# Turning q and k by transposing transfers, and a new order of the weighted sum, the output projection and the sampling

## The chip, the cores and the metric

One core of one Trainium2 chip runs the whole program. The metric is the device time of one execution in microseconds (us). The kernel before took 1519.93 us, the median of 3 runs (1518.76 to 1524.53).

## What is computed

64 sequences of 64 steps and 512 features go through four stages in a row, each added to the running x:

```python
# 1, attention over each sequence, 16 heads of 32
xn = rms_norm(x, g_norm) * (1 + scale) + shift       # scale, shift = cond @ W_emb + b_emb
q, k, v = split_heads(xn @ W_qkv)
q = rms_norm(q, g_q); k = rms_norm(k, g_k)
o = softmax(q k^T * 32**-0.5) v                      # the weighted sum
x = x + o + o @ W_out                                # the output projection
# 2, sampling: between neighbouring features, at positions made from cond,
#    one row of 512 for each of the 64 sequences
i0 = floor(ix); w1 = ix - i0
x = x + (1 - w1) * x[..., i0] + w1 * x[..., i0 + 1]
# 3, a GRU over the steps, and 4, an oscillator (Runge-Kutta, 4 evaluations with a
#    512 x 512 coupling a step) driven by x: 64 steps, one after another
```

## The kernel before, in words

**Stages.** Attention and sampling come first, in `attention_and_sampling`; the two recurrences follow in `recurrences` and are not touched. The 64 sequences are taken in 32 pairs of 128 tokens. Every matrix product is made of float16 pairs (a high and a low part), in three terms, high by high, high by low, low by high; the sampling, whose matrix holds only zeros and ones, has two.

**Slots.** Work is pipelined by hand. Slot i has a fixed list on each engine, in which `pair(d)` is pair i + d: the projections are those of pair i (q, k and v in three banks of psQ), the scores and the softmax those of pair i - 1, the weighted sum and the output projection those of i - 2, and the sampling that of i - 3 (called tap). Slots 0 to 30 are of this kind; the last pair, N0, and what is left of N1 to N3 come after, in lists of their own. Engines meet only at semaphores.

**TensorE (PE)** in a slot (line 1284): `turn_qk` of pair i - 1, eight transposes of 128 x 128 float32 from qn into psA (line 1119); `project` q; `scores`; `project` k; `mix` of the first element (the weighted sum, line 1208); one chunk in four of `project` v; `mix` of the second element; three chunks of `project` v; `proj`, the output projection (line 1228), which writes the bank psO that `mix` wrote; `sample` twice, once for each element of the pair (line 1176); and `turn_rs`, which lays the norms of x along the columns for `scale_x`. `sample` writes psQ's bank 0 or 1, waits for the one-hot matrix (`e_built`), for q's or k's bank to be read out (`qn_done`), and for the copies of x1 (`x1_moved`).

**x1** (one buffer, but for the last three pairs) holds a pair's x after attention, as float16 high and low part, and a second time moved by one row, since sampling takes two neighbouring rows. ACT writes the high part (`high_x1`, line 617), POOL the low part (`low_x1`, line 442), once both samplings of the pair before are through. SP then makes the copy that is moved by one row with three transfers: 112 rows, 15 rows, and the last row from the next chunk (`move_x1`, line 290).

**DVE** (`slot`, line 970) is the busiest of the others: it scales x (`scale_x`, line 756), takes the low part of q and k out of psA (`low_qk`, line 746), builds the one-hot matrices by comparing the positions, broadcast to all partitions, with each partition's index (`build`, line 763, eight instructions of 512 columns a slot), sums squares, takes the least score (`least`), makes the norm exact by one step of Newton's method (`newton`), scales q and k into qn (`scale_qk`, line 801), takes low parts, and weighs the sampled taps (`weigh_taps`, line 858).

**ACT** casts and squares, takes logarithm and exponential for norms and softmax, and writes the high parts (`high_qk`, line 530, with the gain as its scale).

**POOL** (line 463) in a slot: `modulate` of pair i + 1 behind DVE's `scale_x`; `add_taps` of pair i - 4, twice two additions; `low_x1`; `low_x`; then, behind DVE's reciprocals, `norm_p` and `low_halves` of pair i - 1.

**SP** issues the transfers in this order (line 333): `turn_p` twice, transposing transfers that turn the softmax weights of pair i - 2, 128 x 1024 float16 each, in place of work on PE; x of pair i + 3 in two layouts; the first row of positions; `move_x1`; a piece of W_hh or W_ih; the second row. A transfer that waits holds up all behind it.

**Start.** SP first loads cond turned, W_emb, x, cond as it is, then W_qkv. DVE's first work on cond as it is (`grid_front`, line 894, the sampling positions) stands in its list ahead of splitting W_emb into parts (`low_we`).

Of the kernel before, what the change touches and what calls it, by code (L numbers as in the profile page):

```python
# [16 lines left out]
PART = 128  # L17
# [45 lines left out]
def program(nc, x, x_turned, cond, cond_turned, vectors, W_emb, W_qkv, W_out, W_ih, W_hh, coupling_turned, out, rows_dram, wih_dram):  # L63
# [8 lines left out]
    with ExitStack() as ctx:  # L72
# [26 lines left out]
        with ExitStack() as s:  # L99
            attention_and_sampling(nc, ctx, s, block, banks, S, x2_done, x2_first, ts_, first4, XR, condT, ident, Wx, later, x, x_turned, cond, cond_turned,  # L100
                                   vectors, W_emb, W_qkv, W_out, W_ih, W_hh, coupling_turned, rows_dram, wih_dram)
# [4 lines left out]
def attention_and_sampling(nc, sems, ctx, block, banks, S_, x2_done, x2_first, ts_, first4, XR, condT, ident, Wx, later, x, x_turned, cond, cond_turned,  # L106
                           vectors, W_emb, W_qkv, W_out, W_ih, W_hh, coupling_turned, rows_dram, wih_dram):
# [29 lines left out]
    lidx, gqk = sb("lidx", [PART, KC]), sb("gqk", [PART, 1])  # L137
# [12 lines left out]
    qkT = first4[:, :, :, :].rearrange("p a c b -> p (a c b)").bitcast(F16).rearrange("p (i v c n) -> p i v c n", i=2, v=2, c=KC)  # L150
# [3 lines left out]
    S = sb("S", [PART, HEADS, T])  # L154
    mn = sb("mn", [PART, HEADS])
# [5 lines left out]
    rows = [sb(f"rows{u}", [PART, D], F16) for u in range(2)]  # L161
# [18 lines left out]
    i0h = rows[0][0:B, :]  # L180
# [14 lines left out]
    def last_use(eng, p):  # L195
        if p.n == N2.n:
            eng.wait_ge(rs_T, NP)
        elif p.n == N1.n:
            eng.wait_ge(qkv_done, NP * 3)
        else:  # L200
            eng.wait_ge(qk_T, NP)
# [13 lines left out]
    cond_in, condT_in, vectors_in = sem("cond_in"), sem("condT_in"), sem("vectors_in")  # L215
# [17 lines left out]
    qk_T, qk_hi, qk_ready = sem("qk_T"), sem("qk_hi"), sem("qk_ready")  # L233
    sc_done, mn_done, sub_done, exp_done, den_done, rden_done, p_done = (
# [44 lines left out]
    def _(sp):  # L279
# [37 lines left out]

        def store_wih(k):
# [14 lines left out]
        def slot(pair, i):  # L333
# [5 lines left out]
            if i == 2:  # L339
                sp.wait_ge(rows_ready, 1)  # L340
                sp.dma_start(rows_dram, i0h).then_inc(rows_out, 16)
# [14 lines left out]
            if p := pair(-2):  # L356
                load_rows(p, 1)

# [24 lines left out]
    def _(pool):  # L383
# [4 lines left out]
        nc.gpsimd.iota(lidx[:, :], pattern=[[PART, KC]], base=0, channel_multiplier=1,  # L388
# [127 lines left out]
    def _(act):  # L516
# [3 lines left out]
        act.dma_start(vT[:, :], vectors).then_inc(vectors_in, 16)  # L520
        nc.scalar.add_instruction(mybir.InstLoadActFuncSet(name=nc.get_next_instruction_name(), act_func_set_id=LN_EXP_SET))
# [111 lines left out]
        def slot(pair, i):  # L633
            if p := pair(-1):
                high_qk(p, 0)
                high_qk(p, 1)
# [14 lines left out]
            if p := pair(1):  # L651
                high_x(p)
            if i == 1:
                high_cp(1)
                high_wo(0)
                high_wo(1)
            if i > 0:
# [8 lines left out]
            if p := pair(-1):  # L666
                if p.n > 1:
                    exps(p, 2, HEADS)
                    high_halves(p, 0)
                else:  # L670
                    exps_at_once(p)
# [5 lines left out]
            if 0 <= i - WR_FROM < WR_PIECES:  # L677
                high_wr(i - WR_FROM)
            if p := pair(-1):
# [28 lines left out]
        high_qk(N1, 0)  # L708
        high_qk(N1, 1)
# [5 lines left out]
        high_qk(N0, 0)  # L715
        high_qk(N0, 1)
# [24 lines left out]
    def _(dve):  # L741
# [4 lines left out]
        def low_qk(p, n):  # L746
            dve.wait_ge(qk_hi, p.n * 2 + n + 1)
            need(dve, sc_done, p.n)
            t = psA[:, n, :].rearrange("p (c n) -> p c n", c=KC)
            if n == 0:  # L750
                v.scalar_tensor_tensor(out=qkT[:, 1, 0, :, :], in0=t, scalar=gqk[:, 0:1],
                                       in1=qkT[:, 0, 0, :, :], op0=ALU.mult, op1=ALU.subtract)
            else:
                v.tensor_tensor(qkT[:, 1, 1, :, :], t, qkT[:, 0, 1, :, :], ALU.subtract).then_inc(qk_ready, 1)
# [8 lines left out]
        def build(p, b, chunks):  # L763
            if chunks[0] == 0:
                dve.wait_ge(rows_in[b], p.n * 16 + 16)
                if p.n < NP - 1:
                    need(dve, samp_done, p.n * 2 + b - 1)
                elif b == 1:
                    for u in range(2):
                        dve.wait_ge(wih_out[u], 3 * KC // 2 * 16)  # L770
                if p.n == 0:
                    dve.wait_ge(consts, 3)
                    dve.wait_ge(cp_lo, KC)
                    dve.wait_ge(wo_lo, KC)
            for k in chunks:
                e = v.tensor_scalar(E_of(p, b)[:, k, :], rows[b][:, :], lidx[:, k:k + 1], None, ALU.is_equal)  # L776
            if chunks[-1] == KC - 1:
                e.then_inc(e_built, 1)
# [22 lines left out]
        def scale_qk(p):  # L801
            dve.wait_ge(rs_step, (p.n + 3) * STEPS)
            need(dve, qk_T, p.n)
            for n in range(2):
# [1211 lines left out]
```

## Time and profile before

| | |
|---|---|
| median of 3 runs | 1519.93 us |
| the profiled execution | 1523.93 us, span 1522.1 us, TensorE clock 0.994 of full |
| PE matmul busy | 1474.8 us (97%) |
| DVE | 1309.1 us (86%) |
| ACT | 900.4 us (59%) |
| POOL | 762.2 us (50%) |
| POOL's normalisation of the softmax (line 434), mean of 64 | 1.049 us |
| DMA, mean | 55 GB/s, busy in the first 16 of 40 slices |

The span is the time from the first to the last instruction of the profiled execution. An engine's busy time is a share of all stages together; attention and sampling end at about 600 us. Line 518 is ACT's helper for every activation, so that its groups are told apart by tiles. "first" is the tile first4, in which qkT lies; "front" holds x, the squares, the halves and xn; "room" holds the one-hot matrices; "um" the weighed taps.

### The profile page before, as it was taken

The numbers are of one execution on the slowest core, as the hardware profiler recorded it, in microseconds if no ns is written. First come the engines' busy times: TensorE is split into PE (matmuls) and PEld (weight loads), VectorE is DVE, ScalarE is ACT, GpSimd is POOL, SyncE is SP. The second block draws the span as 40 slices with busy tenths as digits, with TensorE's granted clock in tenths as the row PEclk, the third lists the DMA queues.
The fourth block names the chain that finished last, engine by engine and source line by source line (L and its number), as shares of the span: only waits on it lengthen the run. The fifth ranks groups of instructions, "written<-read, shape, count | busy, mean of one in ns | idle before, by whom it ended". The sixth has DMA issues, their size and how long they took to land.

```text
span 1522.1 us, 95000 instructions
## 1 busy us (share of the span) xinstructions
PE 1474.8 (97%) x42214; PEld 1306.2 (86%) x42214; DVE 1309.1 (86%) x3190; ACT 900.4 (59%) x2753; POOL 762.2 (50%) x916
## 2 busy tenths in 40 slices
PE   4899999999999999999999999999999999999997
PEld 2466776667766678999999999999999999999996
DVE  6898888888888887698888888888889888988887
ACT  5566766667666653555555555555555555555553
POOL 2567676776777655443443444344444444434432
PEclk9999999999999999999999999999999999999999
DMA  7255444545455441000000000000000000000000
GB/s 256 55 124 108 108 103 108 118 116 125 120 128 129 93 128 54 8 16 15 12 15 15 15 12 15 15 12 15 15 12 16 15 15 12 15 15 12 15 15 14
DMA packets 122602, 84.03 MB, mean 55 GB/s; under 512 B 68656, under 2 KB 107824, under 8 KB 122192
## 3 DMA queue, kind: packets, MB, share of 16 engines
q1 hardware_dynamic: 121968, 77.87, 20.4%
q8 instruction: 331, 5.42, 1.5%
q14 instruction: 79, 0.65, 0.2%
q10 hardware_dynamic: 224, 0.09, 0.0%
HBM read 42.23 MB, written 11.60 MB: 35 GB/s over the span
## 4 chain that ended last, share of the span: by engine, by line
PE 90%; DVE 4%; issue 2%; POOL 1%; ACT 1%; DMA 0%; SPq 0%; DVEq 0%; ACTq 0%; POOLq 0%
PE psB L1435 34%; PE psA L1464 15%; PE psQ L1146 15%; PE psA L1469 8%; PE psQ L1189 7%; PE psO L1235 5%; PE psO L1223 2%; PE psA L1124 2%; PE psB L1171 2%; POOL S L434 1%; DMA front<-in_cond 0%; DVE psO L1648 0%; DVE den L835 0%; POOL front L453 0%; DVE room L880 0%
## 5 line engine op out<-in xcount | busy, mean ns | idle before, releaser
L1435 PE MATMUL psB<-first,Wx 128*128 128x64 f16 x9216 | 291.3, 193 | 1.7 <-issue 1.1
L1464 PE MATMUL psA<-ts,Cp 128*128 128x64 f16 x8160 | 280.9, 193 | 6.9 <-ACT ts L1535 6.2
L1435 PE MATMUL psB<-first,Whh 128*128 128x64 f16 x9072 | 286.4, 193 | 1.1 <-POOL first L1900 0.5
L1435 PEld LDWEIGHTS psB<-first,Wx 128*128 128x128 f16 x9216 | 278.5, 98 | 2.4 <-issue 1.9
L1146 PE MATMUL psQ<-Wx,front 128*128 128x512 f16 x1152 | 275.0, 385 | 4.3 <-DVE front L952 4.1
L1435 PEld LDWEIGHTS psB<-first,Whh 128*128 128x128 f16 x9072 | 273.9, 98 | 1.8 <-issue 1.1
L1464 PEld LDWEIGHTS psA<-ts,Cp 128*128 128x128 f16 x8160 | 256.3, 98 | 8.3 <-ACT ts L1535 7.0
L1535 ACT ACTIVATE ts<-qst 128x256 f16<-128x256 f32 x192 | 80.1, 417 | 297.1 <-DVE qst L1648 297.1
L1146 PEld LDWEIGHTS psQ<-Wx,front 128*128 128x128 f16 x1152 | 106.7, 99 | 120.6 <-issue 7.7
L1900 POOL TENSOR_TENSOR en<-rz,dn 128x256 f32<-128x256 f32 x64 | 46.7, 729 | 259.5 <-issue 256.7
L1469 PE MATMUL psA<-ts,Cp 128*128 128x64 f16 x4080 | 161.4, 193 | 0.3 <-issue 0.3
L1675 DVE TENSOR_TENSOR ts<-psA,ts 128x256 f16<-128x256 f32 x255 | 107.3, 421 | 47.0 <-ACT psA L1535 47.0
L776 DVE TENSOR_SCALAR room<-rows,lidx 128x512 f16<-128x512 f16 x256 | 144.8, 608 | 0.3
L434 POOL TENSOR_TENSOR S<-S,rden 128x512 f32<-128x512 f32 x64 | 67.0, 1049 | 151.2 <-DVE rden L844 151.2
L1469 PEld LDWEIGHTS psA<-ts,Cp 128*128 128x128 f16 x4080 | 137.0, 98 | 0.6 <-issue 0.4
L518 ACT ACTIVATE S<-psB,mn 128x64 f32<-128x64 f32 x448 | 133.2, 339 | 1.2 <-DVE mn L822 1.2
L1648 DVE SCALAR_TENSOR_TENSOR rest<-cub,psQ 128x256 f32<-128x256 f32 x256 | 106.6, 416 | 7.3
L1648 DVE SCALAR_TENSOR_TENSOR psO<-qst,psO 128x256 f32<-128x256 f32 x253 | 107.1, 423 | 2.1
L1189 PE MATMUL psQ<-x,room 128*128 128x128 f16 x1856 | 108.5, 219 | 0.0
L1189 PEld LDWEIGHTS psQ<-x,room 128*128 128x128 f16 x1856 | 104.9, 98 | 0.1
L518 ACT ACTIVATION_READ_ACCUMULATOR S<-psB,mn 128x1 f32 x448 | 104.4, 233 | 0.0
L1900 POOL TENSOR_TENSOR V<-X3b,first 128x256 f32<-128x256 f32 x64 | 46.9, 733 | 114.2 <-DVE first L1762 113.0
(194 smaller groups left out, 2879.0 us busy)
## 6 DMA issues: line engine op xcount, KB each, us to landing
front<-in_x SPq DMA_DIRECT2D x32, 256.0 KB, 3.1
XR<-in_x_turned SPq DMA_DIRECT2D x32, 256.0 KB, 3.4
rows<-rows_dram SPq DMA_DIRECT2D x64, 128.0 KB, 3.0
out<-ob SPq DMA_DIRECT2D x63, 128.0 KB, 1.7
x<-x SPq DMA_DIRECT2D x29, 224.0 KB
Whh<-in_W_qkv SPq DMA_DIRECT2D x12, 256.0 KB, 7.8
room<-in_W_hh SPq DMA_DIRECT2D x12, 256.0 KB, 2.9
room<-in_W_ih SPq DMA_DIRECT2D x12, 256.0 KB, 2.8
```

The lines of the kernel that those rows point to most:

```text
L434: nc.gpsimd.tensor_tensor(part, part, rden[:, 8 * h:8 * h + 8].unsqueeze(2).broadcast_to([PART, HEADS // 2, T]), ALU.mult)\
L518: return nc.scalar.activation(out, in_, f, **k)
L776: e = v.tensor_scalar(E_of(p, b)[:, k, :], rows[b][:, :], lidx[:, k:k + 1], None, ALU.is_equal)
L1146: last = mm(psQ[:, n, :], xn[p.u][:, i, c, :], Wqkv[:, j, c, n * D:(n + 1) * D], start=(c == 0 and t == 0), stop=(c == KC - 1 and t == 2))
L1189: last = mm(o[:, m, :, :], E_of(p, b)[:, c, m * PART:(m + 1) * PART], x1_of(p)[:, :, i, c, b, :], start=(c == 0 and i == 0), stop=(c == KC ...
L1435: last = mm(o, W_[:, i, c, g * PART:(g + 1) * PART], src[:, j, c, :], start=False, stop=False, skip_group_check=True)
L1464: mm(psF[:, s % 2, m, :], Cp[:, i, c, m * PART:(m + 1) * PART], ts_[:, 0, c, :], start=(c == 0 and m == 0 and i == 0), stop=False, skip_gr ...
L1469: last = mm(psF[:, s % 2, m, :], Cp[:, 0, c, m * PART:(m + 1) * PART], ts_[:, 1, c, :], start=False, stop=(c == KC - 1), skip_group_check= ...
L1535: return nc.scalar.activation(out, in_, f, **k)
L1648: return v.scalar_tensor_tensor(out=flat(out), in0=flat(in0), scalar=scalar, in1=flat(in1), op0=ALU.mult, op1=op1)
L1675: v.tensor_tensor(ts_[:, 1, :, :], th, ts_[:, 0, :, :], ALU.subtract).then_inc(S["ts_ready"], 1)
L1900: return nc.gpsimd.tensor_tensor(flat(out), flat(in0), flat(in1), op)
```

## The change

- **q and k.** DVE now scales q and k into psA rather than qn and multiplies q by a row of gains (new tile `gain_row`); ACT and DVE take high and low part from there into qkh (the room of qn), still in the order of tokens; and SP turns each half with a transposing transfer at the end of its list. PE's `turn_qk` is left for the last pair alone, with `high_qk_turned` and `low_qk_turned`, the old forms.
- **PE's order.** Both `mix` move behind three chunks of v's projection (the second with the fourth chunk ahead of it), and `sample` of the first element comes ahead of `proj`.
- **DVE's and ACT's order.** `low_qk` moves from the next slot to the end of its own; `weigh_taps` of the first element goes ahead of it; `low_wr` and `high_wr` move to the middle of the slot, builds and exponentials are regrouped.
- **One-hot matrices.** The row of positions is kept twice, the second less 128, so that one instruction of 1024 columns builds what two did: four a slot. The row's transfer grows from 128 to 256 KB.
- **Start.** cond as it is comes by ACT's queue, with the gains broadcast to all partitions (128 x 4 KB) ahead of it; DVE's `grid_front` and `gains` wait for all three transfers of that queue.

```diff
@@ SP
         def load_rows(p, b):
             need(sp, e_built, p.n * 2 + b - 1)
-            sp.dma_start(rows[b][:, :], rows_dram[bass.ds(p.n * 2 + b, 1), :].rearrange("a n -> (a n)")
-                         .partition_broadcast(PART)).then_inc(rows_in[b], 16)
+            sp.dma_start(rows[b][:, :, :].rearrange("p c n -> p (c n)"), rows_dram[bass.ds(p.n * 2 + b, 1), :, :]
+                         .rearrange("a c n -> (a c n)").partition_broadcast(PART)).then_inc(rows_in[b], 16)
...
+        def turn_qk(p, n):
+            sp.wait_ge(qk_low, p.n * 2 + n + 1)
+            need(sp, sc_done, p.n)
+            sp.dma_start_transpose(qkT[:, n, :, :, :].rearrange("p i c n -> p (i c) n"), qkh[:, n, :, :].rearrange("p i n -> p (i n)"))\
+                .then_inc(qk_in, 16)
...
             if p := pair(-2):
                 load_rows(p, 1)
+            if i < NP - 1:
+                turn_qk(pair(0), 0)
+                turn_qk(pair(0), 1)
...
-                sp.dma_start(condtok, cond).then_inc(cond_in, 16)
@@ ACT
+        act.dma_start(gains2.rearrange("p v n -> p (v n)"), gains.rearrange("v n -> (v n)").partition_broadcast(PART)).then_inc(vectors_in, 16)
+        act.dma_start(condtok, cond).then_inc(vectors_in, 16)
...
         def high_qk(p, n):
-            act.wait_ge(qk_T, p.n + 1)
-            need(act, sc_done, p.n)
-            o, t = qkT[:, 0, n, :, :], psA[:, n, :].rearrange("p (c n) -> p c n", c=KC)
+            act.wait_ge(qn_done if n else q_gained, p.n * 2 + 2 if n else p.n + 1)
+            need(act, qk_in, p.n * 32)
+            a(qkh[:, n, 0, :], psA[:, n, :]).then_inc(qk_hi, 1)
...
-            if (p := pair(-1)) and p.n > 1:
-                exps(p, 0, 2)
-            if p := pair(-2):
-                high_o(p)
+            if p and p.n > 1:
+                exps(p, 4, 8)
             guess(i + 2, QK_X if pair(2) else QK)
...
+            if p and p.n > 1:
+                exps(p, 8, 13)
+            if p2 := pair(-2):
+                high_o(p2)
+            if p and p.n > 1:
+                exps(p, 13, HEADS)
+            high_qk(pair(0), 0)
+            if p and p.n > 1:
+                high_halves(p, 0)
...
+            high_qk(pair(0), 1)
@@ DVE
         def low_qk(p, n):
             dve.wait_ge(qk_hi, p.n * 2 + n + 1)
+            v.tensor_tensor(qkh[:, n, 1, :], psA[:, n, :], qkh[:, n, 0, :], ALU.subtract).then_inc(qk_low, 1)
...
+            for k in range(2):
+                e = v.tensor_scalar(E_of(p, b)[:, 2 * k:2 * k + 2, :].rearrange("p c n -> p (c n)"), rows[b][:, :, :].rearrange("p c n -> p (c n)"),
+                                    lidx[:, k:k + 1], None, ALU.is_equal)
+            e.then_inc(e_built, 1)
...
+        def scale_qk(p, ns=range(2)):
             dve.wait_ge(rs_step, (p.n + 3) * STEPS)
-            need(dve, qk_T, p.n)
-            for n in range(2):
-                v.tensor_tensor(qn[:, n, :].rearrange("p (h d) -> p h d", d=DH), psQ[:, n, :].rearrange("p (h d) -> p h d", d=DH),
+            to = sq if p.n == NP - 1 else psA
+            for n in ns:
+                v.tensor_tensor(to[:, n, :].rearrange("p (h d) -> p h d", d=DH), psQ[:, n, :].rearrange("p (h d) -> p h d", d=DH),
                                 rs[:, n * HEADS:(n + 1) * HEADS].unsqueeze(2).broadcast_to([PART, HEADS, DH]), ALU.mult)\
                     .then_inc(qn_done, 1)
+                if n == 0 and p.n < NP - 1:
+                    dve.wait_ge(qn_done, p.n * 2 + 1)
+                    v.tensor_tensor(psA[:, 0, :], psA[:, 0, :], gain_row[:, :], ALU.mult).then_inc(q_gained, 1)
...
         def grid_front():
-            dve.wait_ge(cond_in, 16)
+            dve.wait_ge(vectors_in, 48)
...
             if tap:
-                build(tap, 0, (1, 2, 3) if tap.n > 0 else range(KC))
+                build(tap, 0)
...
+            if 0 <= i - WR_FROM < WR_PIECES:
+                low_wr(i - WR_FROM)
+            if tap:
+                build(tap, 1)
             sums_qk(qk, 1)
             means(cols, qk, x)
...
+            newton(i + 2, cols)
+            scale_qk(qk, range(1))
+            if (p := pair(-1)) and p.n > 1:
+                invert_sum(p, 0)
             if p := pair(-2):
                 low_o(p)
-            newton(i + 2, cols)
-            scale_qk(qk)
+            scale_qk(qk, range(1, 2))
...
             if tap:
-                build(tap, 1, (2, 3))
+                weigh_taps(tap, 0)
+            low_qk(qk, 0)
+            low_qk(qk, 1)
@@ PE
         def slot(pair, i):
-            if p := pair(-1):
-                turn_qk(p)
             project(pair(0), 0)
...
             if p := pair(-2):
+                project(pair(0), 2, range(KC - 1))
                 mix(p, 0)
-                project(pair(0), 2, range(1))
+                project(pair(0), 2, range(KC - 1, KC))
                 mix(p, 1)
-                project(pair(0), 2, range(1, KC))
-                proj(p)
             else:
                 project(pair(0), 2)
             if p := pair(-3):
                 sample(p, 0)
+            if p := pair(-2):
+                proj(p)
+            if p := pair(-3):
                 sample(p, 1)
             if p := pair(2):
                 turn_rs(p)
```

In the changed kernel each engine's list still ends with what belongs to the second sampling: DVE's slot ends with `low_v` and `weigh_taps` of the second element, and the next one begins with `scale_x`. POOL's list and the place of `move_x1` in SP's are as before.

## Rows read from the trace of the kernel before

**Rows 1.** Busy time by stretch: from:to, length, each engine's busy time (count), clock, DMA share, GB/s.

```profile
315.28:332.46 17.18, 17.18 (x352) 12.24 (x350) 14.96 (x29) 11.75 (x47) 12.04 (x13) 1.00 0.50 125
...
0.00:38.20 38.20, 16.21 (x136) 9.43 (x136) 23.30 (x45) 19.87 (x38) 8.49 (x18) 0.91 0.75 255
```

**Rows 2.** PE in order of time, slot at 315 us: start, length, instructions, idle before.

```profile
311.70 3.74 PE L1189 MATMUL psQ<-x,room 128*128 128x128 f16 x64
...
315.39 1.04 PE L1124 MATMUL psA<-ident,qn 128*128 128x128 f32 x8
...
316.26 2.75 PE L1146 MATMUL psQ<-Wx,front 128*128 128x512 f16 x12
...
326.21 2.84 PE L1235 MATMUL psO<-oT,Wo 128*128 128x128 f16 x48
...
328.89 3.74 PE L1189 MATMUL psQ<-x,room 128*128 128x128 f16 x64
```

**Rows 3.** DVE in order of time, the same slot.

```profile
315.48 0.69 DVE L847 TENSOR_TENSOR um<-psQ,WT 128x512 f32<-128x512 f32 x1
...
316.09 0.68 DVE L760 TENSOR_TENSOR front<-XR,psB 128x512 f32<-128x512 f32 x1
...
318.45 2.30 DVE L776 TENSOR_SCALAR room<-rows,lidx 128x512 f16<-128x512 f16 x3
```

**Rows 4.** POOL in order of time, the same slot.

```profile
316.84 1.09 POOL L453 TENSOR_TENSOR front<-front,modA 128x512 f32<-128x512 f32 x1 [0.45 <-DVE front L760]
...
322.09 1.15 POOL L447 TENSOR_TENSOR x<-XR,x 128x512 f16<-128x512 f32 x1
...
330.85 2.73 POOL L440 TENSOR_TENSOR front<-S,front 128x512 f16<-128x512 f32 x2
```

**Rows 5.** SP's issues in order of time, that slot and the one at 538 us.

```profile
323.27 1.51 SPq L300 DMA_DIRECT2D x<-x  x2
...
538.35 2.66 SPq L315 DMA_TRANSPOSE PT<-front  x2
...
546.75 1.51 SPq L300 DMA_DIRECT2D x<-x  x2
...
548.30 0.64 SPq L302 DMA_DIRECT2D x<-x  x1
```

**Rows 6.** Busy time by stretch, behind the issues at 538.35 and 546.75.

```profile
542.50:543.00 0.50, 0.50 (x71) 0.50 (x73) 0.50 (x2) 0.47 (x1) 0.50 (x2) 1.00 0.00 0
...
549.80:550.00 0.20, 0.20 (x7) 0.20 (x5) 0.18 (x1) 0.20 (x3) 0.00 (x0) 1.00 0.07 10
...
550.20:550.40 0.20, 0.20 (x7) 0.20 (x5) 0.20 (x1) 0.20 (x3) 0.00 (x0) 1.00 0.00 0
```

**Rows 7.** DMA issues of the whole run: count, KB, us to landing.

```profile
rows<-rows_dram SPq DMA_DIRECT2D x64, 128.0 KB, 3.0
...
out<-ob SPq DMA_DIRECT2D x63, 128.0 KB, 1.7
```

**Rows 8.** Line 776 (build), slots from 60 to 560 us: shortest, median, longest in ns.

```profile
L776 DVE TENSOR_SCALAR room<-rows,lidx x228: 300/533/1449, 75.7 to 559.9; 128x512 f16<-128x512 f16 x114
```

**Rows 9.** DVE and ACT in order of time, the start.

```profile
12.14 0.42 DVE L896 TENSOR_SCALAR um<-front 64x512 f32<-64x512 f32 x1 [7.86 <-DMA front<-in_cond]
...
15.86 2.34 DVE L880 SCALAR_TENSOR_TENSOR room<-Wo,room 128x1024 f16<-128x1024 f32 x2
...
9.57 1.06 ACT L518 ACTIVATE room<-Wo 128x1024 f16<-128x1024 f32 x1 [0.27 <-DMA Wo<-in_W_emb]
```

**Rows 10.** PE in order of time, slots 2 and 3.

```profile
58.22 1.10 PE L1171 MATMUL psB<-first 32*64 32x64 f16 x96 [2.87 <-DVE first L754]
...
59.25 4.45 PE L1146 MATMUL psQ<-Wx,front 128*128 128x512 f16 x12
...
75.83 1.09 PE L1171 MATMUL psB<-first 32*64 32x64 f16 x96 [1.56 <-DVE first L754]
```

**Rows 11.** Busy time by stretch, slot 2.

```profile
59.80:63.80 4.00, 4.00 (x35) 1.43 (x36) 3.96 (x5) 0.27 (x1) 3.92 (x4) 0.63 1.27 158
```

More of the change, by code:

```diff
@@ L60, in need, with program @@
     eng.wait_ge(sem, value)
-def program(nc, x, x_turned, cond, cond_turned, vectors, W_emb, W_qkv, W_out, W_ih, W_hh, coupling_turned, out, rows_dram, wih_dram):
+def program(nc, x, x_turned, cond, cond_turned, vectors, gains, W_emb, W_qkv, W_out, W_ih, W_hh, coupling_turned, out, rows_dram, wih_dram):
     B, T, D = x.shape
@@ L100, in program @@
             attention_and_sampling(nc, ctx, s, block, banks, S, x2_done, x2_first, ts_, first4, XR, condT, ident, Wx, later, x, x_turned, cond, cond_turned,
[L101 removed]
+                                   vectors, gains, W_emb, W_qkv, W_out, W_ih, W_hh, coupling_turned, rows_dram, wih_dram)
         with ExitStack() as s:
@@ L106, in attention_and_sampling @@
 def attention_and_sampling(nc, sems, ctx, block, banks, S_, x2_done, x2_first, ts_, first4, XR, condT, ident, Wx, later, x, x_turned, cond, cond_turned,
-                           vectors, W_emb, W_qkv, W_out, W_ih, W_hh, coupling_turned, rows_dram, wih_dram):
+                           vectors, gains, W_emb, W_qkv, W_out, W_ih, W_hh, coupling_turned, rows_dram, wih_dram):
     B, T, D = x.shape
@@ L160, in attention_and_sampling @@
     x1 = sb("x1", [PART, 2, 2, KC, 2, T], F16)
-    rows = [sb(f"rows{u}", [PART, D], F16) for u in range(2)]
+    rows = [sb(f"rows{u}", [PART, 2, D], F16) for u in range(2)]
     um = [sb(f"um{u}", [PART, KC, 2, T]) for u in range(2)]
@@ L656, in slot @@
                 high_wo(1)
+            p = pair(-1)
+            if p and p.n > 1:
+                exps(p, 0, 4)
             if i > 0:
@@ L761, in scale_x, with build @@
                             rsT.unsqueeze(1).broadcast_to([PART, KC, PART]), ALU.mult).then_inc(xr_done, 1)
[L763 to L778, printed above, removed]
+        def build(p, b):
+            dve.wait_ge(rows_in[b], p.n * 16 + 16)
+            if p.n < NP - 1:
+                need(dve, samp_done, p.n * 2 + b - 1)
+            elif b == 1:
+                for u in range(2):
+                    dve.wait_ge(wih_out[u], 3 * KC // 2 * 16)
+            if p.n == 0:
+                dve.wait_ge(consts, 3)
+                dve.wait_ge(cp_lo, KC)
+                dve.wait_ge(wo_lo, KC)
+            for k in range(2):
+                e = v.tensor_scalar(E_of(p, b)[:, 2 * k:2 * k + 2, :].rearrange("p c n -> p (c n)"), rows[b][:, :, :].rearrange("p c n -> p (c n)"),
+                                    lidx[:, k:k + 1], None, ALU.is_equal)
+            e.then_inc(e_built, 1)
         def means(cols, qk, x):
@@ L917, in grid_rows @@
             dve.wait_ge(grid_step, 8)
-            v.tensor_copy(i0h, i0).then_inc(rows_ready, 1)
+            for c in range(2):
+                last = v.tensor_scalar(i0h[:, c, :], i0, 1.0, float(-c * PART), ALU.mult, ALU.add)
+            last.then_inc(rows_ready, 1)
         def grid_weight():
@@ L2002 @@
         vectors=np.concatenate(vectors, axis=0).T,
+        gains=np.stack([np.tile(inputs[n], D // inputs[n].shape[0]) for n in ("L0_cond_g_q", "L0_cond_g_k")]),
         W_emb=inputs["L0_cond_W_emb"], W_qkv=inputs["L0_cond_W_qkv"], W_out=inputs["L0_cond_W_out"],
```

112 lines of the change are left out of this document (49 added, 63 removed).

## The prediction

> **What bounds the kernel now.** I read the page first: its slices show TensorE (PE) in the nineties almost throughout, and the DMA engines busy only in the first 16 slices of 38 us, where attention and sampling run; the recurrences behind are not touched. Then the busy time by stretch: in one steady slot of the attention stage (one pair of batch elements, 17.18 us) PE is busy for all 17.18 us, DVE for 14.96, ACT for 11.75 and POOL for 12.04, at the full clock [rows 1]. So the slot is PE's, and what PE sheds counts only as long as nothing else then takes longer. For that I followed one slot on each queue [rows 2 to 5]. S marks the end of a slot's second sampling, 315.44 us (311.70 plus 3.74 in [rows 2]).
>
> **The loop to watch** is that of x1, which has one buffer. From S: DVE weighs the last taps (315.48) and scales x (316.09) [rows 3]; POOL starts to modulate at 316.84, adds four taps, and subtracts for x1 from 322.09 to 323.24 [rows 4]; SP issues three copies of x1 one row down, the first at 323.27 [rows 5]; when all have landed PE may sample, which frees the buffer for the next pair. In the kernel before, PE samples at 328.89, 13.45 us behind S, and never waits.
>
> **The change part by part.**
>
> **PE loses the turning of q and k.** From 315.39 to 316.26 it costs 0.87 us a slot [rows 2]. The rest of the slot keeps its matmuls: 17.18 - 0.87 = 16.31 us.
>
> **The copies of x1 now gate PE.** Ahead of the first sampling stood projections, scores, weighted sum and output projection; the output projection (326.21 to 328.89, 2.68 us) now comes behind it. Everything else that stood ahead took 316.26 to 326.21, 9.95 us, and the next slot's project now begins 0.05 us ahead of S (316.26 less 0.87, against 315.44). So PE reaches the sampling 9.9 us behind S. The copies: SP issues the first 323.27 - 315.44 = 7.83 us behind S, as POOL's list is not changed. How long they take no view lists, so I bound it. In a quiet slot the first is issued at 546.75 and the third at 548.30 [rows 5]; the last packets of the three pass in 549.8 to 550.2 [rows 6], 3.05 to 3.45 us behind the first issue. From an issue to landing the quickest transfer of the kernel, the output's, takes 1.7 us and the positions' 3.0 [rows 7]; behind the third issue (1.55) that makes 3.25 to 4.55. I take 4.05, towards the upper end, since in most slots weight loads stand in the same queue. Copies landed: S + 7.83 + 4.05 = S + 11.9, and 0.1 for PE to start. Then both samplings, 3.74 with the tail of the last matmul, with the output projection's 2.68 between them: 6.42 us. The loop is 7.83 + 4.05 + 0.10 + 6.42 = **18.40 us** a slot, against 17.18: +1.22. With the bounds 3.25 and 4.55 it is 17.60 to 18.90. PE has some 2.1 us idle in each slot, and the 0.87 us are worth nothing. The loop closes from slot 3 to slot 30, 27 times: 27 x 1.22 = **+32.9 us** (+11 to +46).
>
> **A second loop of the same length** has POOL in it: DVE now waits for the first sampling (weighing its taps) ahead of the low parts of q and k and the second reciprocal, and behind that reciprocal POOL has a normalisation, 1.05 by the table above, and two subtractions, 2.73 us [rows 4]. From the start of the first sampling: 1.95 for it, 0.6 x 3 on DVE, 0.3 for reciprocal and start, 3.8 on POOL, 7.85 in all; modulation comes at 6.42 + 1.40 = 7.82. It adds nothing, but a faster copy alone would not undo the loss.
>
> **Two transposing transfers a slot on SP,** at the end of its list. A pair of the same size (the weights of attention) is issued from 538.35 for 2.66 us and the data is through by 542.5 [rows 5, 6], 4.2 us on; added SP time 2.7 us a slot, on a queue with 8 us of issues in 17. Queued behind are the next slot's transfers: the pair for the weighted sum (due 8 us into the slot) and loads that are due a slot later. From the start of the first sampling: 1.95 for it, 0.6 for its taps and 0.6 for the low part of q, then the first issue at 3.2 and both halves there at 3.2 + 4.2, some 7.5 us behind the start; scores need them 6.4 + 2.7 = 9.1 behind. Cover 1.6 us, and 2.1 more of PE's idle time. Cost 0. If the cover went, each us late would be a us a slot. Against this stands a rule: by the Trainium skill (VectorE: DVE Perf Modes, The three transpose paths) a transfer takes 1309 ns to turn a 128 x 128 block of 2 bytes and TensorE 390, and TensorE is to be preferred where PSUM will do; with 8 blocks a half, one after another, the slot would be set by turning. This trace disagrees: 16 blocks pass in about 3 us beside others.
>
> **DVE.** One multiplication more (the gain, 128x512 out of PSUM, as the 0.68 of L760 [rows 3]); one of the low parts a little shorter (-0.07); it has 2.2 us idle a slot before and more after. Building the one-hot matrices: 8 instructions of 512 columns become 4 of 1024. Three of them now take 2.30 us beside POOL [rows 3], though one takes 0.30 at its best and 1.45 at its worst [rows 8]: each seems to wait for POOL's current instruction. The Trainium skill (SBUF — State Buffer, SBUF: two separate sides) says that the two engines hold a shared pair of ports for a whole instruction: then half as many would wait half as often, and the first one, longer, could hold back POOL's modulation by 0.15 us, 4 us in all. Without it I put 0; the DVE way from S to the scaled q, with two builds more in it, sums to some 10.5 us behind S and so stays behind the copies' 11.9.
>
> **ACT** turns two reads of PSUM into two of the same kind: 0, under its 5.4 us of idle. Weights' casts moved earlier: 0, same reason. Rows' transfers double to 256 KB, still 3 us, needed 5 us later: 0.
>
> **The start.** DVE stands still until 12.14 us for cond's 128 KB, queued on SP behind the weights, and only then splits W_emb, done at 15.86 + 2.34 = 18.2 us; ACT had its last high part started at 9.57 [rows 9]. On ACT's queue cond lands early, but 512 KB of gains come along, 2 us at the 255 GB/s of this stretch [rows 1]. The split could end at 9.6 + 1.1 + 2 + 1.2 = 13.9: -4.3. W_qkv's pieces land for long after, so I take **-3** (-4.3 to +2).
>
> **Slots 1 and 2, and the end.** They are bound by chains of waits; transfers in place of 0.87 us of turning cost some 3 us more latency, DVE's order gives some back: 0 (-3 to +3). One turning goes from the last slots: **-0.9**.
>
> **Sum** against the profiled execution, 1523.9 us: +32.9 - 3 - 0.9 = +29 us, 1553. The median of the runs shown is 4 us lower, so **1549 us**, +1.9%; by the bounds of the terms 1524 to 1566.
>
> **The rivals.**
> **The kernel gets the PE time back.** If the copies land in 2.1 us rather than 4.05, PE is gapless at 16.31: 27 x -0.87 = -23.5, with start and end -27.4: **1492**. For it: the kernel before never waits for them. Against: the packets last 3 us at least, and the second loop. 0.18, with all mixtures.
> **It evens out.** The loop is at 17.2 to 17.35: copies at about 3 us, in the lower bound of the rows, with the start's gain against the rest: **1516 to 1525**. 0.14.
> **The clock falls in PE's pause.** The granted clock was 0.63 of the 2.4 GHz level in 59.8 to 63.8, so partly the 1.2 GHz one [rows 11], behind 2.87 us of waiting at 58.22; 75.83 came behind only 1.56 us [rows 10]. The 2.1 us lie between. A fall as long as that one would add about 1.7 us to each slot (project took 4.45 at 59.25 [rows 10] in place of 2.75 [rows 2]): 27 x 1.7 = 46, **1595**. 0.06.
> **The transfers that turn are slow.** Where a pair takes up to 3.7 us longer, the pause absorbs it. Three times the 4.2 us, 12.6, puts the halves at 15.8 behind the start of the sampling, 6.7 late, 2.1 of it covered: 27 x 4.6 = 124, **1673**. Against: the pair's 4.2 us held in a stretch with other transfers before and behind it [rows 6]. 0.02. The Trainium skill's figure above would make it 21 us a pair, further out still; this trace has no such row.
> **Forecast** 0.60: 18.40 us a slot, between 1526 and 1572.
>
> **How the numbers follow.** What measurement can tell from no change is about 0.5%, 7.6 us. Faster 0.18; same 0.14; slower 0.60 + 0.06 + 0.02 = 0.68. The range leaves out the lowest part of the faster case (0.13) and the two slow ones at the top (0.07): 1506 to 1574. Its own range of the likeliest case is 1526 to 1572.
>
> **What would show it.** Right: slots of about 18.4 us; in the list of waits PE's weight load for sampling (L1189's successor) idle some 2 us a slot for the transfer of x1, no wait of scores for q and k; DVE's work in the start done 3 us earlier. Wrong: PE at 99% in the steady slots with a period of 16.3 to 16.5, or PE's pause ahead of scores, or ahead of the output projection, or a granted clock under 1 in the steady stage.

## The result, and the profile after

| | before | after |
|---|---|---|
| median | 1520.68 us (4 runs, 1518.76 to 1524.53) | 1614.9 us (4 runs, 1613.15 to 1619.59) |
| ratio, with its 95% interval | | 1.0618 [1.0601, 1.0635] |
| the profiled execution: time, span | 1523.93, 1522.1 us | 1615.49, 1613.7 us |
| TensorE clock, share of full | 0.994 | 0.961 |
| PE, DVE, POOL busy | 1474.8, 1309.1, 762.2 us | 1493.5, 1307.2, 773.2 us |

The change costs 6.2%. The prediction said 1549 us (1506 to 1574): slower, as it was, but by 29 us where it was 94, and the range doesn't hold the result.

One steady slot, from S (the end of the second sampling) to the next S. Busy time by stretch, in the columns of [rows 1]:

```profile
302.87:323.79 20.92, 18.04 (x343) 13.05 (x342) 14.95 (x25) 11.88 (x47) 12.04 (x13) 0.92 0.55 136
```

It is 3.74 us longer than the slot of [rows 1]. PE stands idle for 2.88 us of it, and although it lost the turning it is busy longer, 18.04 us for 17.18, because the clock is at 0.92. DVE, ACT and POOL do as much as before. PE in order of time shows both:

```profile
311.59 0.82 PE L1168 MATMUL psQ<-Wx,front 128*128 128x512 f16 x3
312.35 0.55 PE L1248 MATMUL psO<-PT,Vt 64*32 64x64 f16 x48
315.77 3.55 PE L1214 MATMUL psQ<-x,room 128*128 128x128 f16 x32 [2.88 <-DMA x<-x]
319.14 2.86 PE L1260 MATMUL psO<-oT,Wo 128*128 128x128 f16 x48
321.84 1.95 PE L1214 MATMUL psQ<-x,room 128*128 128x128 f16 x32
```

There is one pause, ahead of the first sampling, and it ends with the transfer of x1. The two samplings are the same 32 matmuls; the first took 3.37 us until the next group began, the second, undisturbed, 1.78. So matmuls run at half pace behind the pause. In [rows 2] both samplings together took 3.74. PE's list of waits over 90 to 640 us (waited for: us in total, times, longest) names this pause and almost nothing else:

```profile
PE psQ L1214 <- DMA x<-x: 67.2, 27, 3.9
PE psB L1196 <- DMA first<-qn: 0.7, 1, 0.7
```

What stands ahead of the transfer, POOL in order of time:

```profile
304.27 1.22 POOL L465 TENSOR_TENSOR front<-front,modA 128x512 f32<-128x512 f32 x1 [0.85 <-DVE front L785]
...
308.13 1.18 POOL L437 TENSOR_TENSOR um<-um 128x256 f32<-128x256 f32 x1
...
310.14 1.33 POOL L459 TENSOR_TENSOR x<-XR,x 128x512 f16<-128x512 f32 x1
```

POOL starts 1.40 us behind S, as before, but takes 7.20 us to the end of `low_x1` (311.47), where it took 6.40 in [rows 4]. SP follows at once, and turns q and k later in the slot:

```profile
311.51 1.50 SPq L304 DMA_DIRECT2D x<-x  x2
313.05 0.64 SPq L306 DMA_DIRECT2D x<-x  x1
...
320.67 2.63 SPq L325 DMA_TRANSPOSE first<-qn  x2
```

From the first issue of the copies (311.51) to PE's start (315.77) it is 4.26 us in this slot; from slot to slot it lies between 3.3 and 4.9.

DVE in order of time, its four wide builds and the scaling of q, which is read out of psQ by 313.84, 10.97 us behind S:

```profile
304.11 1.67 DVE L800 TENSOR_SCALAR room<-rows,lidx 128x1024 f16<-128x1024 f16 x2
...
308.64 1.82 DVE L800 TENSOR_SCALAR room<-rows,lidx 128x1024 f16<-128x1024 f16 x2
...
313.14 0.70 DVE L829 TENSOR_TENSOR psA<-psQ,rs 128x512 f32<-128x512 f32 x1
```

**The account.** S of slot 3 is at 98.42 us (before: 90.41), that of slot 30 at 650.79 (before: 556.11). The early slots cost 8.0 us, the 27 loops (650.79 - 98.42) / 27 = 20.46 us each in place of 17.25, together 86.7 us, and what follows is 3.1 us shorter. 8.0 + 86.7 - 3.1 = 91.6, the difference of the spans. On average over the 27 loops SP issues the first copy 8.62 us behind S, PE begins to sample 3.90 us later, and from there to the next S it takes 7.94 us: 20.46 in all.

The early part in order of time, the first rows DVE and ACT, the others PE:

```profile
9.02 0.42 DVE L923 TENSOR_SCALAR um<-front 64x512 f32<-64x512 f32 x1 [4.62 <-DMA front<-in_cond]
...
11.73 1.06 ACT L530 ACTIVATE room<-Wo 128x1024 f16<-128x1024 f32 x1 [0.23 <-DMA Wo<-in_W_emb]
...
21.31 4.87 PE L1168 MATMUL psQ<-Wx,front 128*128 128x512 f16 x12 [4.07 <-DVE front L981]
...
42.90 1.49 PE L1196 MATMUL psB<-first 32*64 32x64 f16 x96 [3.29 <-DMA first<-qn]
...
73.54 4.40 PE L1260 MATMUL psO<-oT,Wo 128*128 128x128 f16 x48 [5.72 <-DVE oT L892]
...
90.38 3.52 PE L1214 MATMUL psQ<-x,room 128*128 128x128 f16 x32 [1.99 <-DMA x<-x]
```

DVE's work on cond comes at 9.02 rather than 12.14 [rows 9], while ACT's last part of W_emb starts at 11.73 rather than 9.57: the gains delay the weights. Then scores wait for turned q and k, and the output projection of slot 2 waits 5.72 us for DVE.

### The profile page after: what moved, and what is told of

It reads as the page before. It is cut to its first block, busy times and chain, and to the rows that moved or that the text cites. A ratio compares the mean times of both kernels' runs of the same rounds, so it can differ in the third digit from the quotient of the medians.

```text
span 1613.7 us, 94467 instructions
## 1 busy us (share of the span) xinstructions
PE 1493.5 (93%) x41966; PEld 1323.7 (82%) x41966; DVE 1307.2 (81%) x3095; ACT 904.3 (56%) x2753; POOL 773.2 (48%) x916
## 4 chain that ended last, share of the span: by engine, by line
PE 70%; POOL 13%; DVE 5%; DMA 4%; issue 3%; SPq 3%; ACT 1%; ACTq 0%; DVEq 0%; POOLq 0%
PE psB L1459 32%; PE psA L1488 14%; PE psQ L1214 9%; PE psA L1493 7%; PE psO L1260 6%; POOL front L465 4%; DMA x<-x 4%; POOL um L437 3%; SPq L304 3%; POOL XR L440 3%; POOL x L459 2%; DVE front L785 1%; PE psQ L1168 1%; DMA front<-in_cond 0%; POOL S L446 0%
## 5 line engine op out<-in xcount | busy, mean ns | idle before, releaser
L1214 PE MATMUL psQ<-x,room 128*128 128x128 f16 x1856 | 146.3, 252 | 70.0 <-DMA x<-x 70.0
L1214 PEld LDWEIGHTS psQ<-x,room 128*128 128x128 f16 x1856 | 136.8, 115 | 72.4 <-issue 72.3
L874 DVE TENSOR_TENSOR um<-psQ,WT 128x512 f32<-128x512 f32 (+1 forms) x66 | 44.4, 675 | 95.4 <-PE psQ L1214 92.0
L530 ACT ACTIVATE front<-S 128x512 f16<-128x512 f32 x60 | 37.8, 630 | 135.0 <-POOL S L446 134.8
L1260 PE MATMUL psO<-oT,Wo 128*128 128x128 f16 x1536 | 102.9, 233 | 6.0 <-DVE oT L892 6.0
```

Of the source, the lines that this page charges most:

```text
L530: return nc.scalar.activation(out, in_, f, **k)
L1214: last = mm(o[:, m, :, :], E_of(p, b)[:, c, m * PART:(m + 1) * PART], x1_of(p)[:, :, i, c, b, :], start=(c == 0 and i == 0), stop=(c == KC ...
L1260: last = mm(psO[:, m, :], Wo[:, i, c, m * PART:(m + 1) * PART], oT[:, j, c, :], start=(c == 0 and t == 0), stop=(c == KC - 1 and t == 2))
```

## The experiments

Each ratio below is to the kernel before, run beside it on the same chip. "A slot" is the mean of the 27 loops, from S of slot 3 to S of slot 30.

**1. The gate moved nearer: POOL's `low_x1` ahead of `add_taps`,** in the changed kernel.

```diff
@@ POOL
-            for b in range(2):
-                if p := pair(-4):
-                    add_taps(p, b)
...
                 low_x1(p)
+            for b in range(2):
+                if p := pair(-4):
+                    add_taps(p, b)
```

> The changed kernel, with POOL's low part of x1 ahead of the four additions of taps. Theory (the loop through x1, made longer by POOL's chain and by the clock): POOL's low part ends some 3.4 us earlier, at 5.2 behind the end of the second sampling, the copies have landed at 9.5, PE no longer waits for them. What then gates the first sampling is DVE's scaled q, at 11.0 behind: 11.1 + 6.42 = 17.5 us a slot in place of 20.5, a pause of 1.1 us, clock 1.00: 1614.9 - 27 x 3.0 = 1534 us. Rival (the transposing transfers slow the queue and PE waits for them one way or another): the pause moves ahead of the scores, slots of 19 us or more, 1575 us or more.

Measured 1591.01 us, ratio 1.0446 [1.0412, 1.0480], a slot 19.48 us. The gate did move: the copies no longer end the pause. But another wait stood right behind them, as PE's list of waits (90 to 640 us) shows ("psA L829" is DVE's scaled q):

```profile
PE psQ L1214 <- DVE psA L829: 50.0, 26, 3.0
PE psQ L1214 <- DMA x<-x: 4.7, 2, 2.5
```

DVE and PE in order of time, in a slot whose S is at 336.76:

```profile
341.86 1.22 DVE L918 SCALAR_TENSOR_TENSOR room<-room 128x512 f16<-128x512 f32 x1
...
348.77 2.36 PE L1214 MATMUL psQ<-x,room 128*128 128x128 f16 x32 [1.92 <-DVE psA L829]
```

The sampling writes the bank of psQ in which q was projected, and so waits for DVE to scale q out of it. This came 12.0 us behind S, hardly earlier than in the changed kernel (12.9 in the slot shown, 12.5 on average), and the clock still fell: in 200 to 500 us it was 0.93.

**2. The output projection back ahead of both samplings,** in the changed kernel.

```diff
@@ PE
-            if p := pair(-3):
-                sample(p, 0)
             if p := pair(-2):
                 proj(p)
             if p := pair(-3):
+                sample(p, 0)
                 sample(p, 1)
```

> The changed kernel, with the output projection ahead of both samplings again. Theory: the copies are hidden, but the output projection then waits for the low part of o, which DVE takes 12.3 us behind the end of the second sampling: 12.4 + 2.68 + 3.74 = 18.8 us a slot, 27 x 1.7 = 46 us less, 1569 us, with a pause of 2.3 us ahead of the output projection and a clock still under 1. Rival (the new order of PE alone is the fault): slots of 16.3 to 16.6 us, 1505 us or less.

Measured 1694.7 us, ratio 1.1107 [1.1085, 1.1129], a slot 23.13 us. It went far beyond what was expected. PE's waits (90 to 640 us):

```profile
PE psO L1260 <- DVE oT L892: 79.5, 24, 3.5
PE psB L1196 <- DMA first<-qn: 26.6, 23, 3.0
```

DVE in order of time:

```profile
331.26 0.69 DVE L874 TENSOR_TENSOR um<-psQ,WT 128x512 f32<-128x512 f32 x1 [6.95 <-PE psQ L1214]
```

DVE's list weighs the first sampling's taps ahead of the low parts of q and k and of all that follows. With the sampling late, DVE stands idle for 6.95 us, the halves are turned late, and scores wait. POOL's normalisation of the softmax comes late with it, and here it holds `modulate` back: that starts 3.6 us behind S, right behind POOL's two subtractions, in place of 1.4. And `low_o`, which makes the output projection's operand, stands so far down DVE's list that the projection waits up to 3.5 us for it in its earlier place. The orders of PE and of DVE belong together; one can't be judged with the other left as it is.

**3. The kernel before with nothing but the first sampling ahead of the output projection.**

```diff
@@ PE
                 project(pair(0), 2, range(1, KC))
-                proj(p)
...
                 sample(p, 0)
+            if p := pair(-2):
+                proj(p)
+            if p := pair(-3):
                 sample(p, 1)
```

> The kernel before, with the first sampling ahead of the output projection and nothing else. Theory: the loop through x1 is 7.83 + 4.25 + 6.42 = 18.5 us a slot, +1.3 x 27 = +35, 1556 us, with a pause of 1.3 us in which the clock stays at 1. Rival 1 (it takes the transposing transfers and the longer builds for the loop to bind): 1521 us as before. Rival 2 (the clock falls in a pause of any length): 20 us a slot, 1595 us.

Measured 1568.88 us, ratio 1.0282 [1.0256, 1.0308], a slot 18.84 us. So the loop binds without the transposing transfers and the longer builds, which rival 1 denied: this one change of PE's order makes a slot 1.59 us longer, where the whole change makes it 3.21 us longer. What ended PE's pause was the copies in 11 of the 27 slots and DVE's scaled q in 16: the two gates stand side by side here too. The run also shows both outcomes for the clock, in neighbouring slots:

```profile
331.67 3.37 PE L1189 MATMUL psQ<-x,room 128*128 128x128 f16 x32 [1.98 <-DMA x<-x]
334.83 3.09 PE L1235 MATMUL psO<-oT,Wo 128*128 128x128 f16 x48
...
351.93 1.95 PE L1189 MATMUL psQ<-x,room 128*128 128x128 f16 x32 [1.29 <-DVE qn L805]
```

Behind 1.98 us of waiting the sampling took 3.37 us, behind 1.29 us it took its usual 1.95.

**4. The pause filled:** eight matmuls of 512 columns ahead of PE's wait for x1, in the changed kernel. Their result is overwritten.

```diff
@@ PE, in sample
             pe.wait_ge(e_built, p.n * 2 + b + 1)
+            if b == 0 and p.n < N3.n:
+                pe.wait_ge(qn_done, (p.n + 3) * 2 + 1)
+                need(pe, um_done, p.n * 2 - 1)
+                for _ in range(8):
+                    mm(psQ[:, 0, :], Cp[:, 0, 0, 0:PART], Cp[:, 0, 0, :], start=True, stop=True)
```

> The changed kernel, with eight matmuls of 512 columns added ahead of the first sampling's wait for x1; their result is written over by the sampling. They fill some 1.8 us of PE's pause. Theory (the clock falls in the pause and makes the sampling and the output projection slower, inside the loop): clock back to 1.00, the first sampling 1.8 us again, slots of 8.64 + 4.26 + 6.42 = 19.3 us, 27 x 1.15 = 31 us less, 1584 us. Rival (the clock is not in the loop, the slots are long for another reason): 1615 us or more.

Measured 1588.35 us, ratio 1.0413 [1.0382, 1.0444], a slot 19.28 us. PE in order of time:

```profile
342.64 1.89 PE L1207 MATMUL psQ<-Cp 128*128 128x512 f16 x8 [1.11 <-issue]
344.58 1.96 PE L1219 MATMUL psQ<-x,room 128*128 128x128 f16 x32
```

Busy time over 200 to 500 us:

```profile
200.00:500.00 300.00, 282.74 (x5480) 188.15 (x5465) 232.88 (x390) 188.49 (x749) 193.45 (x188) 1.00 0.63 146
```

Useless work is added, and yet each slot is 1.18 us shorter, with the granted clock at 1.00 rather than 0.92. So the clock's fall is in the loop. But the added matmuls are a gate of their own. They may only start when q has been scaled out of its bank, 10.96 us behind S, and they take 1.8 us; in 21 of the 27 slots the sampling then starts with no wait for the copies at all, as in the slot whose S is at 235.34:

```profile
246.41 1.89 PE L1207 MATMUL psQ<-Cp 128*128 128x512 f16 x8 [1.11 <-issue]
248.13 1.95 PE L1219 MATMUL psQ<-x,room 128*128 128x128 f16 x32
```

On average PE begins to sample 12.86 us behind S, 0.34 later than in the changed kernel, and needs 6.42 us from there to the next S, where the changed kernel needs 7.94. The clock's fall is therefore 1.52 us a slot, 27 x 1.52 = 41 us of the loss, and this run gives back 1.52 - 0.34 = 1.18 of it. That the expected 19.3 us came out is in part luck: its 4.26 us for the copies came from one slot, the average is 3.90, and the added matmuls made up the difference.

**5. DVE's way to q shortened:** experiment 1, and `low_wr` moved from the middle of DVE's slot behind `low_v`.

```diff
@@ DVE
-            if 0 <= i - WR_FROM < WR_PIECES:
-                low_wr(i - WR_FROM)
             if tap:
                 build(tap, 1)
...
+            if 0 <= i - WR_FROM < WR_PIECES:
+                low_wr(i - WR_FROM)
```

> The kernel of e1_x1_low_first, with DVE's low part of the recurrent weights (line 918, 1.22 us between the least score and the builds) moved behind v's low part. In e1 the first sampling came 12.0 us behind the end of the second, at DVE's scaled q. Theory (what is left in the loop is DVE's chain to the scaled q, then the clock): the sums of squares of k start when ACT has them, at 7.1 in place of 8.0, so the scaled q is there at 10.6 to 11.0; the pause of PE falls from 2.5 to about 1.2 us, the clock stays at 1, slots of 10.9 + 6.4 = 17.3 us: 27 x 2.7 less than e1's 1591, 1518 us. Rival (the clock falls in shorter pauses too): 18.5 to 19 us a slot, 1550 to 1565 us.

Measured 1546.6 us, ratio 1.0145 [1.0119, 1.0171], a slot 17.68 us. PE's waits (90 to 640 us):

```profile
PE psQ L1214 <- DVE psA L829: 21.2, 20, 1.7
PE psQ L1214 <- DMA x<-x: 10.0, 8, 2.1
```

One of its pauses, in order of time:

```profile
337.82 1.95 PE L1214 MATMUL psQ<-x,room 128*128 128x128 f16 x32 [1.04 <-DVE psA L829]
```

Of experiment 1's 50 us behind DVE 21 are left, and behind 1.04 us of waiting the sampling takes its full-clock time, 1.95 us. One instruction of 0.75 to 1.22 us moved is worth 1.80 us a slot: the wait itself and the clock behind it. The kernel stays short of what was expected, since S of slot 3 is still at 97.3 us and some slots still wait longer (1.75 us at 109 us, with the clock down behind it).

**6. The turning kept, the order put back.** From experiment 5: transfers, wide builds, start and experiment 1's order of POOL stay; PE's order is that of the kernel before less the turning, and ACT's and DVE's follow it.

```diff
@@ PE
-                project(pair(0), 2, range(KC - 1))
                 mix(p, 0)
-                project(pair(0), 2, range(KC - 1, KC))
+                project(pair(0), 2, range(1))
                 mix(p, 1)
+                project(pair(0), 2, range(1, KC))
+                proj(p)
...
                 sample(p, 0)
-            if p := pair(-2):
-                proj(p)
-            if p := pair(-3):
                 sample(p, 1)
@@ DVE
+            if p := pair(-2):
+                low_o(p)
             newton(i + 2, cols)
...
-            if p := pair(-2):
-                low_o(p)
             scale_qk(qk, range(1, 2))
...
-            if tap:
-                weigh_taps(tap, 0)
             low_qk(qk, 0)
...
+            if tap:
+                weigh_taps(tap, 0)
@@ ACT
-            guess(i + 2, QK_X if pair(2) else QK)
-            if p and p.n > 1:
-                exps(p, 8, 13)
             if p2 := pair(-2):
                 high_o(p2)
+            guess(i + 2, QK_X if pair(2) else QK)
             if p and p.n > 1:
-                exps(p, 13, HEADS)
+                exps(p, 8, HEADS)
             high_qk(pair(0), 0)
-            if p and p.n > 1:
-                high_halves(p, 0)
-            elif p:
+            if p and p.n < 2:
                 exps_at_once(p)
             high_qk(pair(0), 1)
+            if p and p.n > 1:
+                high_halves(p, 0)
```

> The changed kernel with its transposing transfers, builds and start kept, and the order taken back: both weighted sums early, output projection ahead of both samplings, low part of o ahead of the scaled q on ACT and DVE, low parts of q and k no longer behind the first sampling's taps, and POOL's low part of x1 and DVE's weights as in e5. Theory (turning by transfers costs nothing by itself, all of the loss is in what was put ahead of what): output projection at 9.9 behind the end of the second sampling, first sampling at 12.6, copies there at 9.5, q and k turned 1.3 us into the next slot and due at 2.7: PE without a pause, 16.31 to 16.5 us a slot, 1614.9 - 27 x 4.05 = 1505 us, about 15 us faster than the kernel before. Rival (the transfers for q and k arrive late, or slow x1's copies): pauses ahead of the scores, slots of 17.2 us or more, 1525 us or more.

Measured 1505.49 us (6 runs), ratio 0.9879 [0.9857, 0.9901], a slot 16.44 us: 1.2% faster than the kernel before. Busy time of one slot:

```profile
325.31:341.74 16.43, 16.43 (x343) 11.47 (x341) 15.06 (x26) 12.04 (x47) 12.40 (x13) 1.00 0.71 184
```

PE at the end of that slot, in order of time:

```profile
335.38 2.84 PE L1258 MATMUL psO<-oT,Wo 128*128 128x128 f16 x48
338.06 3.74 PE L1212 MATMUL psQ<-x,room 128*128 128x128 f16 x64
```

PE has no gap and full clock. A slot is 0.81 us shorter than before (17.25), of which the 0.87 that PE sheds is the source. So in the steady slots the turning by transfers costs nothing and its gain is kept, and the loss lay in the order around it. The wide builds, the new start and POOL's `low_x1` ahead of its additions are in this run too, and whether the gain needs them was not tried. S of slot 3 is at 95.54 us: 5.1 of the 8.0 us of the early slots come even with the old order of PE.

**7. One-hot matrices by eight instructions of 512 columns,** in the changed kernel.

```diff
@@ DVE, in build
-            for k in range(2):
-                e = v.tensor_scalar(E_of(p, b)[:, 2 * k:2 * k + 2, :].rearrange("p c n -> p (c n)"), rows[b][:, :, :].rearrange("p c n -> p (c n)"),
-                                    lidx[:, k:k + 1], None, ALU.is_equal)
+            for k in range(KC):
+                e = v.tensor_scalar(E_of(p, b)[:, k, :], rows[b][:, k % 2, :], lidx[:, k // 2:k // 2 + 1], None, ALU.is_equal)
```

> The changed kernel, with eight builds of 512 columns in place of four of 1024; same transfers, same order. Theory (a build beside POOL holds POOL's next instruction back, and a longer one more: POOL's chain from modulation to the low part of x1 took 7.20 us after and 6.40 before): POOL's chain back to 6.4 to 6.6, slots 0.7 us shorter, 27 x 0.7 = 19 us less, 1596 us. Rival (POOL waits for taps or for ACT, the builds' width is nothing to it): 1615 us; with twice as many waits of DVE, 1625 us.

Measured 1644.36 us, ratio 1.0778 [1.0752, 1.0805], a slot 21.31 us. DVE and POOL in order of time:

```profile
336.61 3.26 DVE L800 TENSOR_SCALAR room<-rows,lidx 128x512 f16<-128x512 f16 x4
...
342.48 2.93 DVE L800 TENSOR_SCALAR room<-rows,lidx 128x512 f16<-128x512 f16 x4
...
341.97 1.60 POOL L459 TENSOR_TENSOR x<-XR,x 128x512 f16<-128x512 f32 x1
```

PE's first wait (90 to 640 us):

```profile
PE psQ L1213 <- DVE psA L828: 69.0, 22, 4.2
```

Half of the reason held. POOL's chain is 6.79 us (336.78 to 343.57) rather than 7.20, with modulation at 1.09 and 1.05 us rather than 1.22 and 1.11. But each group of four builds takes about 3 us in place of the 1.67 and 1.82 of two wide ones, DVE comes late with q, and that decides. The wide builds save some 2.7 us of DVE a slot and cost POOL up to 0.4.

For the rest of POOL's longer chain the changed kernel's own last three slots are a test. DVE has no piece of the recurrent weights left there, that is, no `low_wr`, which the change had moved to the middle of DVE's slot. POOL's second addition of taps takes 0.72 to 0.91 us there in place of 1.18:

```profile
595.47 0.72 POOL L437 TENSOR_TENSOR um<-um 128x256 f32<-128x256 f32 x1
```

The chain is 6.74 us in these slots in place of 7.20, and q is scaled 10.51 us behind S in place of 10.97. In the last three slots of experiment 7, with narrow builds besides, it is 6.40, as in the kernel before. In the kernel before the pieces end at the same slot and its chain doesn't change. So the new place of `low_wr` seems to cost POOL 0.4 to 0.5 us and the width of the builds about 0.4; `low_wr` alone was not put back in the changed kernel.

**8. The kernel before with cond on ACT's queue,** without the gains.

```diff
@@ SP
-                sp.dma_start(condtok, cond).then_inc(cond_in, 16)
@@ ACT
         act.dma_start(vT[:, :], vectors).then_inc(vectors_in, 16)
+        act.dma_start(condtok, cond).then_inc(cond_in, 16)
```

> The kernel before, with cond as it is loaded on ACT's queue in place of SP's; nothing else. Theory (the start waited for it): DVE's first work at 5 us in place of 12, W_emb split by 14, PE's first projection at some 20 us in place of 23.8 (21.3 in the changed kernel, whose gains come ahead), and a part of it kept: 1517 to 1519 us. Rival (the start is bound by W_qkv's pieces or by what the early slots wait for): 1520 us as before.

Measured 1521.0 us (12 runs), ratio 0.9979 [0.9964, 0.9994]: a gain of about 3 us. DVE and PE in the start:

```profile
6.64 0.42 DVE L896 TENSOR_SCALAR um<-front 64x512 f32<-64x512 f32 x1 [2.70 <-DMA front<-in_cond]
...
19.78 4.78 PE L1146 MATMUL psQ<-Wx,front 128*128 128x512 f16 x12 [4.64 <-DVE front L952]
```

The first projection starts at 19.78 us; in the kernel before it was 23.83, in the changed one, with 512 KB of gains on the same queue, 21.31.

## Why the prediction was wrong

**Right:** the loop. PE waits once a slot, for the transfer of x1, ahead of the first sampling, and the 0.87 us it sheds are worth nothing there. Experiment 3 shows the loop binding with nothing else changed. The transposing transfers cost nothing in the steady slots (0.7 us of waiting in 550), and experiment 6 shows their gain kept. The trace thus goes against the rule of the Trainium skill (VectorE: DVE Perf Modes, Rules for kernel authors) that prefers TensorE for turning while PSUM will do: here PE was the bound and the queue had room, and a slot without the turning on PE took 16.44 us in place of 17.25.

The forecast's three terms against their averages over the 27 loops:

| us a slot | forecast | measured | difference |
|---|---|---|---|
| S to the first copy's issue | 7.83 | 8.62 | +0.79 |
| copies, and PE's start | 4.15 | 3.90 | -0.25 |
| from the first sampling's start to the next S | 6.42 | 7.94 | +1.52 |
| a slot | 18.40 | 20.46 | +2.06 |

**The step that failed first: the clock.** The loop was summed at full clock with PE idle for 2.1 us in it, and the fall behind such a pause stood apart as a rival of 0.06. The rows named there left it open: 1.56 us of waiting left the clock up and 2.87 brought it down [rows 10], and the pause lay between. In the runs the pause, 2.5 us on average, slowed the work behind it in 23 of 27 slots. The rival's price, 1.7 us a slot, was near the 1.52 measured; what was wrong was to leave it out of the sum. In the four slots in which the clock stayed up, a slot took 17.93 to 18.41 us. That this is the forecast's 18.40 is luck: a later issue and quick copies, 3.3 us, cancel.

**The second: POOL's chain.** "As POOL's list is not changed" took its time as unchanged. It is 7.20 us in place of 6.40 in all but the last three slots, since the list's neighbours on DVE changed. The price of 0.15 us, set aside for a wider build ahead of modulation, looked at one instruction alone, and `low_wr`, now beside the chain, had no price at all. By experiment 7 and the last slots each is about half of the 0.8.

**The copies** were a little quicker than forecast, within its bounds.

**Slots 1 and 2** were put at 0 (-3 to +3) and the start at -3. PE's first projection came 2.5 us earlier, but S of slot 3 8.0 us later, so some 10.5 us went in between. Experiment 6 leaves 5.1 of the 8.0 to the part that is not PE's order (scores wait for the halves there too); in experiment 3 PE's order alone makes 1.7. Where chains of waits bound a slot, a transfer's latency counts in full, and the cover that I counted in steady slots is not there.

**DVE's scaled q** was put at 10.5 us behind S; it ended at 10.97, the 0.46 more being the `low_wr` on its way, and, covered by the copies, cost nothing. Experiment 1 made it the gate at once. The "second loop" through POOL's normalisation never set a slot of the changed kernel; in experiment 2 it did hold POOL back.

**The end** gave 3.1 us, forecast 0.9. What gave the rest was not tried.

**The sum.** From the forecast's 1553 us for the profiled execution: 27 x 2.06 = +56, start and early slots +11 (8.0 later where 3 earlier was forecast), the end -2: 1618, measured 1615.49; 2 of the 2.5 us between come from the slot of [rows 1], 17.18 us, taken for the mean of 17.25. The forecast's bounds, added straight up, make 1523 to 1570 rather than "1524 to 1566", which changes nothing here.

## What to carry to other kernels

A pause in TensorE is not paid by its length alone. Where the new loop leaves PE idle for some 2 us a slot, sum the work behind the pause at the lower clock as well, and give that sum a weight of its own in the forecast. And before an operation is moved ahead on the bounding engine, list everything it waits for, with each one's time behind the slot's start: here the copies of x1 came 12.5 us behind S and the bank of q 11.0, so moving the one nearer uncovered the other. Work that fills a pause is a gate too: ask when it may start and how long it takes before reading the result. And a change that relieves the bound and one that reorders it should be timed apart: with PE's old order the kernel was 1.2% faster, with the new one 6.2% slower.

## What the runs showed of the hardware

- **A pause and the clock.** Filling a pause with eight useless matmuls made the kernel 2% faster: ratio 1.0413 in place of 1.0618. The length of a pause alone did not decide whether the clock fell. Ahead of the first sampling, in the changed kernel and in experiments 1, 3, 5 and 7, pauses of up to 1.7 us left it at 1.95 us and those above 2.1 us slowed it; between 1.75 and 2.1 us both happened, as in the changed kernel (the first two lines) and in experiment 1 (the third):

```profile
133.23 1.95 PE L1214 MATMUL psQ<-x,room 128*128 128x128 f16 x32 [1.97 <-DMA x<-x]
192.51 3.27 PE L1214 MATMUL psQ<-x,room 128*128 128x128 f16 x32 [1.89 <-DMA x<-x]
191.67 1.95 PE L1214 MATMUL psQ<-x,room 128*128 128x128 f16 x32 [2.06 <-DVE psA L829]
```

- **Two engines in SBUF.** Comparing 1024 columns takes DVE about 0.9 us beside POOL, comparing twice 512 about 1.5, and POOL's modulation beside the wide ones lasts 0.13 and 0.06 us longer (experiment 7). It fits what the Trainium skill (SBUF — State Buffer, SBUF: two separate sides) says, that the two engines hold a shared pair of ports for a whole instruction; no run here shows the ports themselves.
- **Broadcast rows.** The row of 256 KB landed in 4.4 us, that of 128 KB in 3.0 [rows 7]; the prediction had left it at 3:

```profile
rows<-rows_dram SPq DMA_DIRECT2D x64, 256.0 KB, 4.4
```
